# Picking a sixth of the gathered source rows by one-hot products on TensorE, with byte masks and fewer products in a graph network kernel

## Time and profile before

| what | value |
|---|---|
| median of three runs | 1410.02 us |
| profiled execution, whole | 1406.4 us |
| its span, first to last instruction | 1404.6 us |
| TensorE busy | 1145.8 us, 82% |
| VectorE busy | 951.3 us, 68% |
| GpSimd busy | 753.6 us, 54% |
| ScalarE busy | 661.6 us, 47% |
| mean granted TensorE clock | 0.74 of 2.4 GHz |

### The profile page before, as it was taken

How to read it: one execution, slowest core, us unless ns; L and a number is a source line. 1 busy time by engine, 2 the same in 40 slices (tenths; PEclk the granted TensorE clock), 3 DMA queues, 4 the chain that set the end, 5 groups by cost and what they waited for, 6 DMA issues and landing times.

```text
span 1404.6 us, 43341 instructions
## 1 busy us (share of the span) xinstructions
PE 1145.8 (82%) x16938; PEld 818.6 (58%) x16938; DVE 951.3 (68%) x3140; ACT 661.6 (47%) x1910; POOL 753.6 (54%) x793
## 2 busy tenths in 40 slices
PE   3279999999977888788878878878766895999995
PEld 2235555555544554455445545555455795999995
DVE  7277777777776667666766666667444999555555
ACT  1146666666655556555555555556501992000000
POOL 5777777777777777777777777777300000000000
PEclk9556677777666666766666667666758898999998
DMA  4521111112111111111111111110000000000000
GB/s 102 80 54 45 41 39 38 38 37 53 44 38 37 37 38 37 37 37 37 38 37 37 37 38 36 40 37 14 9 1 2 3 4 2 4 4 4 4 4 16
DMA packets 51171, 43.63 MB, mean 31 GB/s; under 512 B 34562, under 2 KB 47202, under 8 KB 50962
## 3 DMA queue, kind: packets, MB, share of 16 engines
q1 hardware_dynamic: 25938, 27.95, 6.9%
q0 software_dynamic: 25024, 12.86, 6.4%
HBM read 38.18 MB, written 2.57 MB: 29 GB/s over the span
## 4 chain that ended last, share of the span: by engine, by line
PE 34%; POOL 31%; DVE 17%; issue 12%; DMA 3%; SPq 1%; ACT 1%; ACTq 0%; DVEq 0%
POOL arena L485 31%; PE ps L681 15%; PE ps L638 7%; DVE arena L1242 6%; PE ps L597 2%; PE ps L621 2%; DVE arena L1088 2%; PE ps L605 2%; DVE arena L1086 1%; PE ps L592 1%; DMA arena<-x_pad,arena 1%; SPq L406 1%; DMA arena<-line_table 1%; DMA dst_parts<-arena 1%; DVE arena L1101 1%
## 5 line engine op out<-in xcount | busy, mean ns | idle before, releaser
L485 POOL DMA_INDIRECT arena<-x_pad,arena x782 | 751.8, 961 | 238.6 <-issue 236.4
L638 PE MATMUL ps<-arena,mix 128*32 128x80 f32 x1666 | 243.6, 320 | 0.6 <-ACT arena L845 0.6
L1088 DVE TENSOR_SCALAR arena<-pair_no,arena 128x275 bf16<-128x275 f16 (+2 forms) x784 | 239.4, 309 | 0.0
L605 PE MATMUL ps<-arena 128*128 128x275 bf16 (+1 forms) x784 | 156.9, 336 | 100.6 <-DVE arena L1088 100.1
L681 PE MATMUL ps<-arena,adj_words 128*128 128x64 f16 (+1 forms) x6875 | 215.8, 193 | 28.0 <-DVEq L1280 16.2
L681 PEld LDWEIGHTS ps<-arena,adj_words 128*128 128x128 fp8e4 x6875 | 213.2, 98 | 30.9 <-DVEq L1280 17.3
L638 PEld LDWEIGHTS ps<-arena,mix 128*32 128x32 f32 x1666 | 224.3, 147 | 4.5 <-ACT arena L845 1.0
L1101 DVE TENSOR_TENSOR arena<-ps,arena 128x132 f32<-128x132 f32 x196 | 57.1, 291 | 248.2 <-DMA arena<-x_pad,arena 133.1
L597 PE MATMUL ps<-arena 1*128 1x500 bf16 (+1 forms) x392 | 172.2, 440 | 30.5 <-DVEq L1064 20.7
L1116 DVE TENSOR_TENSOR arena<-ps,arena 128x768 f32<-128x768 f32 x196 | 187.9, 959 | 6.7
L621 PE MATMUL ps<-arena 128*32 128x187 f32 x1568 | 137.9, 435 | 21.2 <-DVE arena L1116 18.8
(11 more groups left out here) (187 smaller groups left out, 1243.5 us busy)
## 6 DMA issues: line engine op xcount, KB each, us to landing
arena<-line_table SPq DMA_DIRECT2D x28, 602.0 KB
arena<-x_pad,arena POOLq DMA_INDIRECT x782, 2.6
arena<-line_table SPq DMA_DIRECT2D x28, 140.0 KB
arena<-dst_parts SPq DMA_DIRECT2D x196, 5.7 KB
dst_parts<-arena SPq DMA_DIRECT2D x1, 918.8 KB, 11.5
feat_table<-rows SPq DMA_DIRECT2D x1, 800.0 KB, 13.8
x<-x_pad SPq DMA_DIRECT2D x1, 400.0 KB
out<-x SPq DMA_DIRECT2D x1, 400.0 KB, 4.9
```

What stands on the lines that cost most here:

```text
L485: pool.indirect_dma_start(to, None, table, bass.IndirectOffsetOnAxis(ap=index, axis=0)).then_inc(done, 16)
L605: mm = nc.tensor.matmul(ps[:, at + first:at + first + n], row_hot[:, h, k, :], pair_hot[:, h, k, 0:n], start=False, stop=(k == SLOTS - 1))
L638: mm = nc.tensor.matmul(ps[0:FEAT, MOVED:MOVED + BATCH * PAGE], mix[:, m, :], sumsT[:, c % 2, :, m], start=(m == 0), stop=(m == MIXES - 1))
L1088: last = v.tensor_scalar(pair_hot[:, h, k, 0:n], pair_no[:, 0:n], pair_of[:, g, k:k + 1], None, ALU.is_equal)
```

## The change

- **Picked rows.** In every third group (3, 6, ..., 192: 64 groups) the last two tiles are no longer gathered. Their source numbers, less multiples of 128, are stored once as `src_table` (float16); SP broadcasts one line of it (256 KB) per picked group, VectorE turns it into one-hot operands (`make_src_hot`), TensorE multiplies these with three bf16 parts of x (`pick`, 24 products of 192 or 224 columns), and VectorE selects and adds one of seven column sets into `xp` (`select_picks`). The ring of gathers becomes 14 groups deep instead of 21.
- **Products.** The clearing products of `count` and `sum_mixed` are gone; `count` uses eight products in place of four to start fresh columns. `times_bases` exchanges its operands: the 80 strided columns of `sumsT` are stationary, the 32 columns of `mix` stream, and its result has nodes as partitions.
- **Layer-1 sums.** ScalarE copies that result to `agg_rows`; SP stores each page to `agg_table` in HBM, one after the other, and two loads bring all of it back to `agg`. `to_nodes` and `to_agg` are gone, and ScalarE's second move of each page.
- **ScalarE** makes two one-hot rows instead of one.
- **Masks.** VectorE compares into bytes (0 or 255) for 17 blocks, ScalarE takes a sign for the other 8, and VectorE joins each with `adj` by a bitwise AND on 782 words. The `adj` products of the softmax go from 50 to 25 a block, with 66 columns, into banks of their own. Out-degree sums are spread over earlier waits of ScalarE.

```diff
-AHEAD = 21
+AHEAD = 14
 SIDES = 14
 PAGES = 8
-DELAY = BATCH + 2
+DELAY = 2
+ROW_PAGES = 6
+STORE_DELAY = SIDES + 10
+SRC_LINE_DELAY = 6
-ROWS_BY_SCALAR = 1
+ROWS_BY_SCALAR = 2
+PICK_EVERY, PICKS = 3, 2
+LOW, HIGHS = 4, 7
+LOW_BITS = 9
+SRC_LINES = 2
...
-ADJ_MAX = 16
+ADJ_MAX = 8
...
+PICKED = [g for g in range(PICK_EVERY, GROUPS, PICK_EVERY) if (g + 1) * SLOTS <= TILES]
...
+        def gathered_tiles(g):
+            return min(SLOTS - PICKS if g in PICKED else SLOTS, TILES - g * SLOTS)
...
+                def load_src_line(g):
+                    n = PICKED.index(g)
+                    if n >= SRC_LINES:
+                        sp.wait_ge(picks_out, n - SRC_LINES + 1)
+                    sp.dma_start(src_lines[:, n % SRC_LINES, :], src_table[g:g + 1, :].to_broadcast([P, LOW * PICKS * P]))\
+                      .then_inc(src_line_in[n % SRC_LINES], 16)
+
+                def store_rows(g):
+                    c, n = g // BATCH, g % BATCH
+                    base = sp.value_load(base_t[0:1, g:g + 1], min_val=0, max_val=NODES_PAD - PAGE)
+                    sp.wait_ge(moved_copied, c + 1)
+                    if g >= 1:
+                        sp.wait_ge(rows_paged, 16 * g)
+                    sp.dma_start(agg_table[bass.ds(base, PAGE), :], agg_rows[n * PAGE:(n + 1) * PAGE, c % ROW_PAGES, :])\
+                      .then_inc(rows_paged, 16)
...
+                    if g - SRC_LINE_DELAY in PICKED:
+                        load_src_line(g - SRC_LINE_DELAY)
+                    if g >= STORE_DELAY:
+                        store_rows(g - STORE_DELAY)
+                for g in range(GROUPS - SRC_LINE_DELAY, GROUPS):
+                    if g in PICKED:
+                        load_src_line(g)
+                for g in range(GROUPS - STORE_DELAY, GROUPS):
+                    store_rows(g)
+                sp.wait_ge(rows_paged, 16 * GROUPS)
+                sp.dma_start(agg[:, 0:BLOCKS - 1, 0:FEAT], agg_table[0:(BLOCKS - 1) * P, :].rearrange("(b p) f -> p b f", p=P))\
+                  .then_inc(agg_loaded, 16)
+                last = rows_of(BLOCKS - 1)
+                sp.dma_start(agg[0:last, BLOCKS - 1, 0:FEAT], agg_table[(BLOCKS - 1) * P:NODES, :]).then_inc(agg_loaded, 16)
...
-                for t in range(g * SLOTS, min((g + 1) * SLOTS, TILES)):
+                for t in range(g * SLOTS, g * SLOTS + gathered_tiles(g)):
...
+                    counted_to = 1 if g else 0
                     for k in range(SLOTS):
-                        first, n = STARTS[k] * BLOCKS, min(PAIR_DSTS[k], WIDTH) * BLOCKS
-                        mm = nc.tensor.matmul(ps[:, at + first:at + first + n], row_hot[:, h, k, :], pair_hot[:, h, k, 0:n],
-                                              start=False, stop=(k == SLOTS - 1))
+                        first, end = STARTS[k], STARTS[k] + min(PAIR_DSTS[k], WIDTH)
+                        for d0, d1 in ((first, counted_to), (counted_to, end)):
+                            if d1 > d0:
+                                mm = nc.tensor.matmul(ps[:, at + d0 * BLOCKS:at + d1 * BLOCKS], row_hot[:, h, k, :],
+                                                      pair_hot[:, h, k, (d0 - first) * BLOCKS:(d1 - first) * BLOCKS],
+                                                      start=(g == 0 and k == 0), stop=(k == SLOTS - 1 and d1 == end))
+                        counted_to = end
                     if g + 1 < GROUPS:
                         if g >= 1:
                             pe.wait_ge(counts_copied, g)
                         to = COUNTS + (g + 1) % 2 * BANK
-                        clear(to, PAIRS)
                         mm = nc.tensor.matmul(ps[:, to:to + BLOCKS], row_hot[:, h, SLOTS - 1, :],
-                                              pair_hot[:, h, SLOTS - 1, WIDTH * BLOCKS:HOTS * BLOCKS], start=False, stop=False)
+                                              pair_hot[:, h, SLOTS - 1, WIDTH * BLOCKS:HOTS * BLOCKS], start=True, stop=False)
                     mm.then_inc(pairs_used, 1)
 
                 def sum_mixed(g):
...
                         first = STARTS[q] * MIXES
                         mm = nc.tensor.matmul(ps[q * FEAT:(q + 1) * FEAT, at + first:at + first + WIDTH * MIXES],
                                               xp[:, u, q, 0:FEAT], mixed[:, h, q, 0:WIDTH, :].rearrange("p d m -> p (d m)"),
-                                              start=False, stop=True, tile_position=(0, q * FEAT))
+                                              start=True, stop=True, tile_position=(0, q * FEAT))
                     if g + 1 < GROUPS:
                         if g >= 1:
                             pe.wait_ge(sumsT_copied, g)
-                        to = MIXED + (g + 1) % 2 * BANK
-                        clear(to, PAGE * MIXES)
-                        q = SLOTS - 1
+                        to, q = MIXED + (g + 1) % 2 * BANK, SLOTS - 1
                         mm = nc.tensor.matmul(ps[q * FEAT:(q + 1) * FEAT, to:to + MIXES], xp[:, u, q, 0:FEAT],
-                                              mixed[:, h, q, WIDTH, :], start=False, stop=False, tile_position=(0, q * FEAT))
+                                              mixed[:, h, q, WIDTH, :], start=True, stop=True, tile_position=(0, q * FEAT))
                     mm.then_inc(mixed_used, 1)
+
+                def pick(g):
+                    n = PICKED.index(g)
+                    pe.wait_ge(src_hot_ready, n + 1)
+                    if n >= 1:
+                        pe.wait_ge(picks_read, n)
+                    for k in range(PICKS):
+                        for low in range(LOW):
+                            rows_in = x_parts[:, :, low::LOW, :]
+                            at, cols = PICKED_AT + k * HIGHS * FEAT, len(range(low, BLOCKS, LOW)) * FEAT
+                            for j in range(3):
+                                mm = nc.tensor.matmul(ps[:, at:at + cols], src_hot[:, n % SRC_LINES, low, k * P:(k + 1) * P],
+                                                      rows_in[:, j], start=(low == 0 and j == 0),
+                                                      stop=(low == LOW - 1 and j == 2))
+                    mm.then_inc(picks_out, 1)
...
-                        mm = nc.tensor.matmul(ps[0:FEAT, MOVED:MOVED + BATCH * PAGE], mix[:, m, :], sumsT[:, c % 2, :, m],
+                        mm = nc.tensor.matmul(ps[0:BATCH * PAGE, MOVED:MOVED + FEAT], sumsT[:, c % 2, :, m], mix[:, m, :],
                                               start=(m == 0), stop=(m == MIXES - 1))
                     mm.then_inc(moved_out, 1)
 
-                clear(COUNTS, PAIRS)
-                clear(MIXED, PAGE * MIXES)
+                for bank in range(2):
+                    nc.tensor.matmul(ps[:, MIXED + bank * BANK:MIXED + bank * BANK + PAGE * MIXES], nothing[:, 0:P],
+                                     nothing[:, 0:PAGE * MIXES], start=True, stop=True)
...
+                    if g + 2 in PICKED:
+                        pick(g + 2)
...
-                pe.wait_ge(soft_parts_ready, 2)
+                pe.wait_ge(soft_parts_ready, 1)
                 for b in range(BLOCKS):
                     for j in range(BLOCKS):
-                        for h in range(2):
-                            nc.tensor.matmul(ps[0:rows_of(j), soft_at(j) + SOFT:soft_at(j) + 2 * SOFT],
-                                             adj[:, b, j * P:j * P + rows_of(j)], minus_small[:, b, h, :],
-                                             start=False, stop=False)
+                        nc.tensor.matmul(ps[0:rows_of(j), all_at(j):all_at(j) + 2 * SOFT], adj[:, b, j * P:j * P + rows_of(j)],
+                                         soft_parts[:, b, :, 1, :], start=False, stop=False)
...
+                def copy_moved(c):
+                    act.wait_ge(moved_out, c + 1)
+                    if c >= ROW_PAGES:
+                        act.wait_ge(rows_paged, 16 * BATCH * (c - ROW_PAGES + 1))
+                    a.copy(agg_rows[:, c % ROW_PAGES, :], ps[0:BATCH * PAGE, MOVED:MOVED + FEAT]).then_inc(moved_copied, 1)
...
+                    if n == 2 and c >= 1:
+                        copy_moved(c - 1)
...
+                first, second, third = DEGREES_BEFORE
+                out_degrees(0, first)
                 root(1)
+                out_degrees(first, second)
                 root(2)
+                out_degrees(second, third)
...
+                for n, b in enumerate(BY_SCALAR):
+                    if n >= 2:
+                        act.wait_ge(above_ready, BY_SCALAR[n - 2] + 1)
+                    a.activation(mask_signs[:, 2 + n % 2, 0:NODES], score_row[:, 0:NODES], ACT.Sign, bias=least[:, b:b + 1],
+                                 scale=-1.0).then_inc(scalar_masks, 1)
+                    if n >= 1:
+                        out_degrees(done, done + 1)
+                        done += 1
+                out_degrees(done, BLOCKS)
...
```

(61 more changed lines are left out.)

144 lines of the change are left out of this document (81 added, 63 removed).

## The result

The changed kernel takes **1760.81 us** (median of 4 runs, 1756.84 to 1764.39) where the kernel before takes 1410.6: a ratio of 1.248, 95% interval 1.245 to 1.252. The prediction was 1388 us, 1308 to 1425; the kernel is 25% slower. The profiled execution has a span of 1758.7 us.

What follows compares the result with a forecast made beforehand. Gathers were taken to bound the sweep from about 360 us, with TensorE and VectorE's pace just under. From 1404.6 us, -3 (sweep), -3 (layer-1 sums) and -12 (softmax) gave 1386.6, with 1.8 around it 1388 us; range 1308 to 1425.

Steps and rivals of the forecast that it cites:

- start: Sweep start: the line for group 3, queued behind the second pair of line loads, costs 0 to 12 us, taken as 5.
- The rival with the stores: Layer-1 sums: serial stores fall behind on SP's queue, +15 us on the main case, 1403 us; chance 0.05.
- Pace of the sweep, 4.71 us a group: Sweep: 4.96 us a group at the lower clock, 4.54 at the full one; six tenths at full clock taken.
- the wait behind times_bases: Sweep: score_edges idles for a fetch behind times_bases on TensorE, 3.4 us each, three in 12 groups.
- Gathers removed: Sweep: 654 gathers instead of 782, 4.2 us a group, putting GpSimd's bound just below the TensorE and VectorE one.
- times_bases exchanged, 4.7 to 4.8 us: Basis products in the sweep: exchanged operands keep about 0.14 us an instruction, 4.7 to 4.8 us, no change.
- rival A: Sweep: times_bases gets cheap, 2.3 to 3 us; total 1280 to 1345 us, centre 1320; chance 0.28.
- rival B: Sweep: TensorE stays at the lower clock as the new times_bases no longer raises it; 1435 to 1455 us; chance 0.17.
- Layer-1 sums, -3: After the sweep: four chained stores and a load take 16 us where 19.6 us passed before; -3 us.
- Masks and softmax, -12.4: Softmax blocks: TensorE bounds 25 blocks at 2.66 us, 66.5 us in place of 84.7; -12.4 us after additions.
- rival C: Softmax masks: byte compare runs at one element a cycle; main case plus 13 us, 1401 us; chance 0.1.
- the +1 and +3.6: Softmax: four more closing products cost +1 us, the longer combination at the end +3.6 us.

Runs made afterwards that it cites:

- delay of two: Changed kernel with SRC_LINE_DELAY = 2 instead of 6, so SyncE issues a picked group's source line in pass g+2: 1416.95 us, ratio 1.0045.
- the two cures: Changed kernel with picks' source lines issued in pass g+2 and times_bases cut into three parts (6, 6 and 5 products): 1336.3 us, ratio 0.949.
- every fourth group: Kernel with source lines in pass g+2 and times_bases in parts, but every fourth group picked instead of every third: 1318.69 us, ratio 0.9355.

## Why the prediction was wrong, point by point

**The step that failed** is the one on the queue. I priced the new source lines only at the **start** ("the line for group 3 is queued behind the second pair of line loads ... 0 to 12 us, I take 5"), where it took 9.81 us, and took it for a singular case. It comes back at every line load, since SyncE's hold for the line buffer is not a matter of the start. The kernel before held that queue just as well; only side loads, issued up to 14 groups ahead, stood behind it, so it cost nothing and I read no row of it. The row was there, in the waits of the kernel before:

```profile
SPq L424 <- PE ps L592: 603.0, 26, 28.0
```

The rival with the stores fell on the same queue, and was priced at +15 at its end only. No term of the sum asked, for each DMA added to the queue: what is ahead of it that waits, and in which pass is it wanted? SRC_LINE_DELAY = 6 against a hold of 8 groups' lead, known from the code alone, would have given it: wanted in pass G-9, let go in pass G-9. With the 16 us behind the line loads, which only the later traces gave, that is 28 x 12 us = 336 us where I had 5; with the lines in time the kernel was 343.9 us faster.

**Pace of the sweep, 4.71 us a group.** To be read where the lines are in time (delay of two): (1031.8 - 79.0)/195 = 4.89. Some inputs were off. The granted clock was 0.72 from 200 to 1000 us, so 0.44 of the time at 2.4 GHz where I took 0.6: 4.96 - 0.44 x 0.42 = 4.78. And the reduction of the picks took 0.94 us, not 0.64: four in 12 groups, +0.1. Together 4.88. The structure of the sum, VectorE's own work plus waits behind times_bases plus pick, holds; that the agreement is so close is partly luck. The compare of a pick took 0.48 us, not 0.3 (+0.06 a group), and the wait behind times_bases was 137.1/49 = 2.8 us and not 3.4 (-0.15). With these the sum gives 4.79, and the 0.1 up to 4.89 is not placed.

The Trainium skill (SBUF — State Buffer, Door 1: The DMA port swizzle) has each access that crosses to a new 16-byte line pay a penalty. The trace agrees: the reduction read at 128 bytes and paid 0.32 us, and the product that wrote at 28 bytes paid 0.35. I weighed that rule for times_bases and not for the reduction.

**Gathers removed.** Right: no wait for `x_pad`, 654 gathers.

**times_bases exchanged, 4.7 to 4.8 us.** Nearly right: 4.94 to 4.98 us in the changed kernel, so no change of pace with the exchange; rival A is out.

**The clock, rival B.** It neither stayed at the lower level, as in rival B, nor rose to 0.8, as I had it. Without picks it was 0.54 to 0.58 in the windows after 200 us, with picks 0.72, where the kernel before had 0.66 to 0.70: the picks bring it back. That the new times_bases lets it fall fits the stretch of the delay of two shown above, where the granted clock was 0.50 during the pick (613 to 616 us), 1.00 from 617.1 to 619 and 0.50 again from 620, with times_bases still running; but the run without picks differs from the kernel before in its clearing and counting products too, and no run separates these.

**Layer-1 sums, -3.** From the last copy of times_bases to the first use of the sums it took 10.9 us (1384.12 to 1395.03) instead of 19.6: -8.7. The stores were not behind at the end, and four of them with the load took less than 16 us.

**Masks and softmax, -12.4.** From there to the end 363.7 us against 371.4: -7.7. The stretch of the blocks in the groups view:

```profile
L1359 DVE TENSOR_SCALAR arena<-arena 128x3125 uint8<-128x3125 f32 x15 | 27.7, 1850 | 8.4 <-PE ps L797 7.6
...
L1379 DVE TENSOR_TENSOR arena<-arena,adj_words 128x782 int32<-128x782 int32 x17 | 16.4, 968 | 1.7 <-PE ps L797 1.7
L1370 DVE SCALAR_TENSOR_TENSOR arena<-arena,adj_words 128x782 int32<-128x782 int32 x8 | 8.3, 1032 | 0.0
```

Both prices held, 1.85 for the compare (I had 1.8; rival C is out) and 0.97 for the AND, and VectorE waits for TensorE. A block took 2.76 us, not 2.66 (2.5 us over 25 blocks); the other 2 us of the difference I have not placed. The two parts together were -16.4 us, forecast at -15; that they agree is partly luck, since one gave 5.7 us more and the other 4.7 less. And rival C was priced too low: its 3.3 us a block for 25 blocks, with the +1 and +3.6, makes +2 to +4 against the kernel before, not +1.

## What to carry to other kernels

When a DMA is added to a queue that is programmed in order, write down for it the pass in which it is issued, the pass in which it is wanted, and every wait and every large transfer ahead of it; a wait that cost nothing (603 us of SyncE's queue in the kernel before) makes the first load behind it late, once that load has no lead of its own. Urgent loads go ahead of the held one, or onto another queue. And where two bounds lie close together, try the two cures together: here each alone lost time or gained nothing, and both gave 4% (1394 us to 1336), with every fourth group 5% (1319).

## What the runs showed of the hardware that I had not expected

- A load of 256 KB, 3.1 us by itself, was in use 16.3 to 17.1 us after 742 KB had been issued ahead of it on the same queue. A 2.5 KB store behind 742 KB on the same queue was followed by the next one after 12.7 and 13.7 us; with those loads issued by ScalarE 1.2 us ahead of the store, after 5.7.
- A stride on 448 float32 elements cost VectorE 0.32 us on the reading side (128 bytes) and 0.35 on the writing side (28 bytes).
- The kernel before took 1703 us instead of 1410 in one batch of runs, though nothing in it had changed, and the three kernels run beside it were slower by 12 to 14% than in the repeat. The record has it on another chip (12) than the other batches of experiments (15, 7 and 10). Its three traces alone put waits down to a releaser called "remote", as in `DVE arena L1214 <- remote: 170.4, 40, 7.3`. Why is open, and no time of that batch carries a conclusion above.
